# An explicit order of the attention words, a second order for the drain, and products of ones ahead of the experts

## The reference

```
x = x + layernorm(attention(layernorm(x)))
x = x + layernorm(ffn(layernorm(x)))
```

## Time and profile before

| | us |
|---|---|
| median of the runs shown | 1472.06 |
| the profiled execution | 1470.54 |
| its span, first to last instruction | 1468.8 |
| PE busy | 1219.1 (83%) |
| DVE busy | 954.1 (65%) |
| ACT busy | 721.2 (49%) |
| POOL busy | 836.0 (57%) |
| mean granted TensorE clock | 0.922 |
| chain that ended last | PE 56%, DVE 17%, POOL 8%, issue 8% |

### The profile page before, as it was taken

One profiled execution on the slowest core, in us unless ns is written; L12 is line 12 of the kernel. 1 busy time (PEld: TensorE's weight loads), 2 busy tenths in 40 slices (PEclk: granted clock), 3 DMA queues, 4 the chain that ended last, 5 costly groups with the idle time before them and its releaser, 6 DMA issues.

```text
span 1468.8 us, 27636 instructions
## 1 busy us (share of the span) xinstructions
PE 1219.1 (83%) x8581; PEld 700.7 (48%) x8581; DVE 954.1 (65%) x2397; ACT 721.2 (49%) x1521; POOL 836.0 (57%) x1047
## 2 busy tenths in 40 slices
PE   1479998989989898899988989988549999999920
PEld 0344554454554554545545455453325555555510
DVE  6388887778778677787777766752324444444467
ACT  0116665656556555565555564645214444444424
POOL 5425556657667476675756645545634555555557
PEclk9759999999999999999999998998668999999965
DMA  2431322321332213322132121431022334333256
GB/s 75 122 95 35 109 76 87 85 79 56 97 91 75 79 56 103 89 70 80 58 108 90 55 77 53 106 96 38 28 68 67 92 99 118 99 94 90 84 157 199
DMA packets 135287, 126.18 MB, mean 86 GB/s; under 512 B 17192, under 2 KB 126186, under 8 KB 130538
## 3 DMA queue, kind: packets, MB, share of 16 engines
q1 hardware_dynamic: 115360, 100.27, 23.9%
q0 software_dynamic: 8704, 18.11, 3.8%
q10 hardware_dynamic: 11082, 6.05, 1.6%
HBM read 78.12 MB, written 45.42 MB: 84 GB/s over the span
## 4 chain that ended last, share of the span: by engine, by line
PE 56%; DVE 17%; POOL 8%; issue 8%; ACT 3%; another core or an unknown queue 2%; DMA 1%; SPq 1%; POOLq 0%; DVEq 0%; ACTq 0%
PE wide L1556 6%; PE wide L1448 6%; DVE mx L1230 6%; PE score L1411 6%; PE heads_ps L1421 5%; PE wide L1538 4%; PE wide L1386 4%; PE score L1399 4%; PE score L1528 3%; POOL values L797 3%; PE wide L1557 2%; PE wide L1450 2%; DVE s_h L1171 2%; PE wide L1479 2%; ACT values L926 2%
## 5 line engine op out<-in xcount | busy, mean ns | idle before, releaser
L926 ACT ACTIVATE values<-score 128x512 f32<-128x512 f32 (+1 forms) x704 | 372.4, 558 | 250.6 <-PE score L1411 228.1
L1230 DVE TENSOR_REDUCE mx<-wide 128x2 f32<-128x1024 f32 (+3 forms) x384 | 390.1, 1038 | 127.7 <-PE wide L1450 113.1
L797 POOL TENSOR_SCALAR_AFFINE_SELECT values<-values 128x512 f32<-128x512 f32 x256 | 170.6, 670 | 321.7 <-ACT values L926 319.6
L1448 PE MATMUL wide<-qk 72*128 72x512 bf16 (+3 forms) x1024 | 248.1, 310 | 18.1 <-DVE mx L1230 15.9
L1411 PE MATMUL score<-qk 75*128 75x512 bf16 (+3 forms) x1024 | 241.1, 306 | 14.4 <-ACT values L926 10.7
L1421 PE MATMUL heads_ps<-values 128*32 128x512 f32 (+3 forms) x2048 | 194.1, 452 | 38.1 <-POOL values L797 37.1
L852 POOL DMA_INDIRECT token_scratch<-spread,e_id x144 | 140.9, 978 | 134.8 <-DVE spread L1275 81.8
L1450 PE MATMUL wide<-maskneg,identb 128*128 128x128 bf16 x1024 | 201.5, 225 | 0.0
L1411 PEld LDWEIGHTS score<-qk 75*128 75x128 bf16 x1024 | 82.5, 98 | 159.3 <-ACT values L926 73.9
L786 POOL DMA_INDIRECT sorted_scratch<-zr,places x128 | 131.7, 1029 | 27.3 <-issue 25.4
L1448 PEld LDWEIGHTS wide<-qk 72*128 72x128 bf16 x1024 | 103.1, 101 | 90.9 <-DVE mx L1230 37.1
(11 more groups left out here) (174 smaller groups left out, 1990.5 us busy)
## 6 DMA issues: line engine op xcount, KB each, us to landing
qk<-parts_scratch SPq DMA_DIRECT2D x192, 192.0 KB
parts_scratch<-spread SPq DMA_DIRECT2D x16, 768.0 KB, 8.4
qk<-sorted_scratch SPq DMA_DIRECT2D x144, 66.0 KB
front<-token_scratch SPq DMA_DIRECT2D x16, 512.0 KB, 4.1
xt<-attn_x SPq DMA_DIRECT2D x16, 256.0 KB, 8.7
xr<-attn_x SPq DMA_DIRECT2D x16, 256.0 KB, 8.9
x_scratch<-z SPq DMA_DIRECT2D x16, 256.0 KB, 4.6
shared_scratch<-s_out SPq DMA_DIRECT2D x16, 256.0 KB, 2.3
```

The costliest lines, as they stand in the source:

```text
L797: nc.gpsimd.affine_select(out=prob[n][:, :, 0:P], in_=prob[n][:, :, 0:P], compare_op=ALU.is_ge, fill=0.0, base=0, pattern=[[0, HG], [1, P] ...
L926: nc.scalar.activation(free_ap(prob[kb][:, hs_[0], :], [[1, N * len(hs_)]]), score[SCORE_RING.buffer(b, step)][:, 0:N * len(hs_)], ACT.Exp ...
L1230: nc.vector.tensor_reduce(mx[:, h0:h0 + len(hs_), j:j + 1], src, axis=AX.X, op=ALU.max).then_inc(p1_max, 1)
L1448: nc.tensor.matmul(o, q4[e][0:ROWS, h, j * P:(j + 1) * P], k4[e][0:ROWS, h, 0:L], start=True, stop=False)
```

## The change

The strings of `SLOTS` become one list, `ORDER`, with the group and number of each word spelled out and an offset of its own behind an @ where it differs. Iteration 16, which is now the last, follows a list of its own, `DRAIN`, in which the words of batches 14 and 15 stand in one sequence. The tables become words of that list (`counts`, `blocks`, `ends`, `rows`) and stand ahead of the last batch's shared expert; they use `heads_ps` and the score tiles and no longer the wide ones. SP stores the tails when the first of them is there and waits for the last ahead of the block loads.

The split of the maxima is done ahead of the transpose: DVE works on 128 x 32, PE brings the three bf16 parts across with three products with the identity, and ACT copies them to `mparts`. The bias of V is taken off V, multiplied with `Wp` and added to `bp` once at the start, so V's copy moves from DVE to ACT. `xnT` gets a third buffer. The fills of `k4` move from POOL to DVE, ahead of its wait for the weights, and the loads of expert weights from ACT's queue to SP's. The block tables and `e_xT` become views of `xnT`.

Ahead of the first expert block PE does 32 products of `onesb` with 512 columns, which nobody reads, and another 16 behind the wait for the first block's rows.

```diff
-SLOTS = [
-    "s0 last_v s1 X V last_heads s2 s3 late_p Q cos mask0 Y v0 s4 W s5 K s6 late_p sin0 s7 place sin1 late_p mask1 s8 "
-    "s9 U0 mask2 mask3 late_p G0 H0 v1 s10 zstats zrstd M1 v2",
-    "s0 s1 sin2 mask0 p s2 s3 p v3 d0 mask1 s4 s5 U1 sin3 p G1 s6 mask2 H1 v0 s7 mask3 Z p d1 s8 p s9 heads d2 stats s10 "
-    "v1 v2",
-    "s0 p p s1 U2 s2 p residual G2 s3 s4 p R mask0 H2 rstats s5 s6 v3 p p s7 s8 heads mask1 v0 s9 p p v1 rrstd s10 M0 "
-    "p mask2 rnormal T d3 mask3 v2",
-    "s0 s1 v3 p normal s2 s3 rX s4 p D rstd mask0 s5 p mask1 third0 s6 d4 third1 choose s7 v0 rL second p d5 mask2 s8 "
-    "heads mask3 p s9 d6 p chosen rexp s10 d7 v1 v2",
-]
-LATE = " ".join(SLOTS).split().count("late_p")
...
-FIRST, LAST = -4, 1
+ORDER = (
+    "sin0 s0.0 v3.2@-1 sin1 v3.3@-1 mask0.1 s0.1 X s0.2 chosen@-2 sin2 heads3@-1 p20@0 Q sin3 mask0.2 s0.3 s0.4 "
+    "p21@0 K s0.5 p22@0 d0 cos d1 s0.6 place s0.7 Y v0.0 s0.8 p23@0 s0.9 W mask0.3 s0.10 s1.0 U0 V v0.1 s1.1 M1@0 "
+    "zrstd zstats stats G0 s1.2 p0 v0.2 H0 s1.3 p1 mask1.0 residual v0.3 Z s1.4 U1 R s1.5 d2 p2 v1.0 G1 s1.6 p3 "
+    "s1.7 p4 s1.8 s1.9 p5 rstd s1.10 heads0 s2.0 p6 d3 s2.1 U2 rstats s2.2 G2 mask1.1 p7 s2.3 mask1.2 T v1.1 s2.4 "
+    "mask1.3 rrstd s2.5 second mask2.0 v1.2 p8 s2.6 p9 rnormal mask2.1 v1.3 s2.7 p10 mask2.2 s2.8 p11 v2.0 s2.9 "
+    "s2.10 third0 v2.1 s3.0 M0 normal H1 p12 p13 s3.1 v2.2 s3.2 mask2.3 rX mask3.0 heads1 s3.3 p14 s3.4 rL choose "
+    "v2.3 s3.5 s3.6 third1 H2 rexp mask3.1 p15 mask3.2 p16 mask3.3 v3.0 d4 s3.7 p17 s3.8 d5 heads2 s3.9 p18 s3.10 "
+    "p19 v3.1 d6 D d7 mask0.0@1 "
+)
+DRAIN = (
+    "v3.2@-1 v3.3@-1 chosen@-2 heads3@-1 K place Y d0 d1 W d2 d3 zstats U0 zrstd Z G0 U1 residual G1 rstats U2 "
+    "rrstd G2 rnormal rX rL choose rexp d4 d5 d6 d7 H0 H1 H2 D chosen K@-1 counts@-1 place@-1 blocks@-1 d0@-1 "
+    "d1@-1 d2@-1 d3@-1 d4@-1 d5@-1 d6@-1 d7@-1 U0@-1 ends@-1 U1@-1 rows@-1 U2@-1 G0@-1 G1@-1 G2@-1 H0@-1 H1@-1 "
+    "H2@-1 D@-1 "
+)
+OFFSET = dict(stats=4, rstd=4, normal=4, X=3, Q=3, cos=3, sin=3, R=3, T=3, second=3, third=3, V=1, p=1, M=1, s=0, v=0,
+              mask=0, heads=0, Y=-1, W=-1, zstats=-1, zrstd=-1, Z=-1, residual=-1, rstats=-1, rrstd=-1, rnormal=-1,
+              rX=-1, rL=-1, choose=-1, rexp=-1, chosen=-1, K=-2, place=-2, U=-2, G=-2, H=-2, D=-2, d=-2)
+FIRST, LAST = -4, 0
+GROUPED = ("s", "v", "mask", "heads")
...
+def schedule(text):
...
-        xnT = [sb(f"xnT{n}", [P, NT * P]) for n in range(2)]
+        xnT = [sb(f"xnT{n}", [P, NT * P]) for n in range(3)]
...
-        mrest = sb("mrest", [NH // 2 * NT, P])
+        mrest = sb("mrest", [P, NH // 2 * NT])
+        mpre = [sb(f"mpre{n}", [P, NPART, NH // 2 * NT], BF16) for n in range(2)]
+        bv_all = view(prob[3], F32, [P])
...
-            for n, v in enumerate((bq, bk, bv)):
+            for n, v in enumerate((bq, bk)):
+            sp.dma_start(bv_col[:], bv.rearrange("(h o) -> h o", o=1)).then_inc(weights_in, 16)
...
+                if i == B - 2:
+                    sp.wait_ge(qk_transposed, B)
+                    sp.dma_start(w2_sb[:, :, 0, :], w2[:, 0:HALF, :].rearrange("e h d -> h e d")).then_inc(w2_in, 16)
+                    sp.dma_start(w2_sb[:, :, 1, :], w2[:, HALF:, :].rearrange("e h d -> h e d")).then_inc(w2_in, 16)
+                if i == B - 1:
+                    sp.wait_ge(p2_scores, (B - 1) * P2_N * NG)
+                    sp.dma_start(w13_sb[:, :, 0:INTER], w1.rearrange("e d h -> d e h")).then_inc(w13_in, 16)
+                    sp.dma_start(w13_sb[:, :, INTER:], w3.rearrange("e d h -> d e h")).then_inc(w13_in, 16)
...
+            sp.wait_ge(p_done, 4)
...
-                if i == -3:
-
-                    pool.wait_ge(x_rstd, 1)
-                    for n in range(2):
-                        nc.gpsimd.memset(k4[n][64:96, :, :], 1.0).then_inc(rows_filled, 1)
-                        pool.wait_ge(rows_filled, n + 1)
-                for step in STEPS:
+                for step in (STEPS if i < B else REST):
...
+                    elif step.what == "M":
+                        act.wait_ge(max_transposed[n], b + 1)
+                        wait(act, m_in[n], 16 * NPART * b)
+                        nc.scalar.activation(mparts[n][:], misc[0:NH // 2 * NT, 0:NPART * P].rearrange("p (r c) -> p r c", r=NPART),
+                                             ACT.Copy).then_inc(m_ready[n], 1)
...
+                    elif step.what == "V":
+                        act.wait_ge(v_made, b + 1)
+                        if b == 0:
+                            act.wait_ge(filled, 4)
+                        wait(act, pv_done, (b - 1) * NG * NT)
+                        nc.scalar.activation(free_ap(vext[e][:, 0, 0, :], [[NH * 32, NT], [32, NH], [1, HS]]),
+                                             free_ap(unit[:, 0, :], [[P, NT], [HS, NH], [1, HS]]), ACT.Copy).then_inc(v_ready, 1)
-                        wait(act, v_made, b - 1)
-                        wait(act, qk_made, b)
-                        nc.scalar.activation(xnT[e][:], unit[:, 0, :], ACT.Copy).then_inc(xnT_ready, 1)
+                        wait(act, v_made, b - 2)
+                        wait(act, qk_made, b - 2)
+                        nc.scalar.activation(xnT[b % 3][:], unit[:, 0, :], ACT.Copy).then_inc(xnT_ready, 1)
...
+            for n in range(2):
+                nc.vector.memset(k4[n][64:96, :, :], 1.0).then_inc(rows_filled, 1)
+            nc.vector.tensor_copy(bv_all, free_ap(bv_col[:], [[0, P]])).then_inc(bv_spread, 1)
+            dve.wait_ge(bv_projected, 1)
+            nc.vector.tensor_tensor(bp_bc[:], bp_bc[:], misc[:, 0:P], ALU.add).then_inc(bp_folded, 1)
...
+            def tails_and_blocks():
+                nc.vector.tensor_tensor(tail_row[:], heads_ps[:, P:P + E], region[:], ALU.add).then_inc(p_done, 1)
...
+            def rows_and_experts():
...
-                    elif step.what == "V":
-                        dve.wait_ge(v_made, b + 1)
-                        wait(dve, pv_done, (b - 1) * NG * NT)
-                        nc.vector.tensor_tensor(
-                            free_ap(vext[e][:, 0, 0, :], [[NH * 32, NT], [32, NH], [1, HS]]),
-                            free_ap(unit[:, 0, :], [[P, NT], [HS, NH], [1, HS]]),
-                            free_ap(bqkv_bc[:], [[0, NT], [HS, NH], [1, HS]], 2 * P), ALU.add).then_inc(v_ready, 1)
...
-                        dve.wait_ge(max_transposed[n], b + 1)
-                        wait(dve, m_in[n], 16 * NPART * b)
-                        mt, mp = misc[0:NH // 2 * NT, 0:P], mparts[n]
-                        ms[n].did(nc.vector.tensor_scalar(mp[:, 0, :], mt, -1.0, None, ALU.mult))
+                        dve.wait_ge(p1_max, b * P1_N + (n + 1) * P1_N // 2)
+                        wait(dve, max_transposed[n], b)
+                        m, mp = mx[:, n * NH // 2:(n + 1) * NH // 2, :].rearrange("p h t -> p (h t)"), mpre[n]
+                        ms[n].did(nc.vector.tensor_scalar(mp[:, 0, :], m, -1.0, None, ALU.mult))
...
-                        nc.vector.tensor_tensor(mp[:, 2, :], mrest[:], mp[:, 1, :], ALU.subtract).then_inc(m_ready[n], 1)
+                        nc.vector.tensor_tensor(mp[:, 2, :], mrest[:], mp[:, 1, :], ALU.subtract).then_inc(m_split[n], 1)
...
+                    elif step.what == "counts":
+                        pe.wait_ge(heads_copied, B * NG)
+                        counts = chosen[B % 2][:, NK, :]
+                        nc.tensor.matmul(heads_ps[0:E, 0:1], counts, onesb[:, 0:1], start=True, stop=True)
+                        nc.tensor.matmul(heads_ps[:, P:P + E], onesb[:], counts, start=True, stop=True).then_inc(p_total, 1)
+                    elif step.what == "ends":
+                        pe.wait_ge(p_blocks, 1)
+                        pe.wait_ge(p_done, 1)
+                        nc.tensor.matmul(heads_ps[0:E, 2 * P:2 * P + 1], upto[:], nblk_b[:], start=True, stop=True).then_inc(p_ends, 1)
+                    elif step.what == "rows":
+                        pe.wait_ge(p_past, 1)
+                        pe.wait_ge(exp_done, B * NG * P2_N)
+                        pe.wait_ge(s_out_ready, B - 1)
+                        for o, w in ((score[0], onesb[0:E, :]), (score[1], spare_b[:])):
+                            last = nc.tensor.matmul(o[:, 0:NBLK], w, past[:], start=True, stop=True)
+                        last.then_inc(p_experts, 1)
...
-                        pe.wait_ge(p1_max, b * P1_N + (n + 1) * P1_N // 2)
-                        apart(pe)
-                        nc.tensor.transpose(misc[0:NH // 2 * NT, 0:P],
-                                            mx[:, n * NH // 2:(n + 1) * NH // 2, :].rearrange("p h t -> p (h t)"),
-                                            ident[:]).then_inc(max_transposed[n], 1)
+                        if b == 0 and n == 0:
+                            pe.wait_ge(bp_folded, 1)
+                        pe.wait_ge(m_split[n], b + 1)
+                        for r in range(NPART):
```

(25 more changed lines are left out.)

105 lines of the change are left out of this document (37 added, 68 removed).

## The result

| | before | after |
|---|---|---|
| median, us (7 runs each) | 1467.08 | 1452.04 |
| profiled execution | 1470.54 | 1447.03 |
| its span | 1468.8 | 1445.3 |
| PE / DVE / ACT / POOL busy in it | 83 / 65 / 49 / 57% | 84 / 67 / 51 / 57% |

The ratio is 0.9906 (95% interval 0.9883 to 0.9928): the gain is clear of the noise, but under the 2% from which two kernels are called different, so the verdict is "same". Some executions of either kernel fall in a slower state (1689 and 1695 us of the seven before); they stay in the medians and out of the ratios. Forecast was 1434; the time lies in the range, the gain is under half of the forecast one. The profiled execution of after is the fastest of its seven, so its span is 23.5 shorter where the medians differ by 15.

The account below looks back on a forecast made before the run. PE bounds the loop only in part: 5.3 us of a batch idle, mostly behind POOL's masks and DVE's maxima. 1470.5 - 32 (loop) - 2.5 (start) - 3.3 (entry) = 1432.7; the median lies 1.5 higher: 1434, range 1390 to 1473.

Parts of the forecast that it names:

- The loop, -2.3 a full batch: Attention loop: -1.2 from DVE, -1.6 from POOL, +0.5 for D make -2.3 us a full batch, -32 in all.
- A batch that still takes 60: Sign in the loop that the forecast is wrong; copies out of the shared experts were to come every 58.4 us.
- D at the end, 0.5 given back: Shared experts' down product, last in the order, keeps PE busy 3 us with one exp queued on ACT: +0.5 a batch.
- rival (D): Slower: in the loop D holds PE, the next score waits for its copy; 3 a batch, 1507 us, chance 0.10.
- POOL, -1.6: Loop: of 2.6 us a batch that PE idles behind POOL's masks, 1.6 goes as masks stand ahead of scatters.
- DVE, -1.2 of 1.9: Loop: smaller splits and V's bias take 1.9 us a batch off DVE; 1.2 of PE's idle comes back.
- PE's work stays: Loop: PE does the same words; three bf16 products replace each f32 transpose of the maxima, +0.1 a batch, within rounding.
- The last batches, -8.0: Batch 12's first exp to the last value product's end: 2.8 full batches and one lighter, -8.0 us in all.
- The start, -2.5: Start: k4 fills on DVE, two taking 14.1 us by elements; first normalisation ends at 25.0 against 27.5, -2.5.
- Drain and entry, -3.3: Last value product to first expert blocks: blocks in 7.2 us earlier, first transpose -1.4, faster first blocks -1.9.
- The products of ones: Ahead of the first expert block: 32 cost 6.9 us and 16 cost 3.5 at full clock, and buy 1.9.
- (C): Rival for the loop: waits only move and the lighter DVE alone counts; 1457 us, up to 1472, chance 0.30.

Follow-up runs that it names:

- a1: The changed kernel itself, unchanged, on another chip, with no signal late: 1390.3 us, 0.960 of the kernel before.
- e1: The changed kernel with D (shared experts' down product and its copy) two scores earlier in the repeated order: 1408.9 us, 0.975 of the kernel before.
- e5: The changed kernel with the old order written out as the list, on the chip where the kernel before takes 1470: 1590.2 us, 1.085 of it.
- e2: The changed kernel with scatters d4 to d7 spread over GpSimd's idle stretches, D left last: 1413.5 us, 0.979 of the kernel before.
- e3: The changed kernel with U1 moved ahead of the residual and normal behind rX: 1372.5 us, 0.951 of the kernel before.
- e4b: e4 run once more, on the chip of a1: 1382.3 us, 0.955 of the kernel before.
- e4: The changed kernel with the two k4 fills on VectorE as 4096 4-byte words each instead of 8192 2-byte ones: 1381.1 us, 0.955 of the kernel before.
- c2: c1 with another drain list (H0 to H2 earlier among the scatters, K of the last batch ahead of D): 1359.1 us, 0.941 of the kernel before.
- c1: The changed kernel with the edits of e3 and e4 together, run twice: 1362.7 and 1363.1 us, 0.942 and 0.946 of the kernel before.
- a0: The changed kernel itself once more, on the chip where the kernel before takes 1470: 1455.3 us, 0.992 of the kernel before.
- b0: The kernel before, unchanged, once more, on the same chip as a0: 1469.7 us.
- b1: The kernel before, unchanged, on a chip without late signals: 1441.7 us, one execution.

## Why the forecast was off

**The loop, -2.3 a full batch, came out at +0.1 in the result (60.7 to 60.8).** This is the step that failed, by two of its terms: D, given 0.5, and the gain of a lighter DVE, given 1.2. Without late signals 2.3 came (58.6 to 56.3), but that the number fits is luck, for the terms came out otherwise than written: 2.6 instead of 1.6 from POOL, 0.6 from a wait for exps that the sum didn't have, nothing for D, and 0.9 lost behind the maxima where 1.2 was to be won. A batch that still takes 60 is what the forecast named as its own sign of being wrong.

*D at the end, 0.5 given back.* This term failed by its size. PE idled 2.6 to 2.8 behind D in seven of the nine full batches from 252 to 799, and the clock fell behind it. The forecast had this in rival (D), with its place and its price of 3 a batch, but weighed it at 0.10; the copy alone takes 0.6. What made it 2.8 is PE's late signals. They are in the trace of before too, where ACT's copy `oT` waited for a value product long ended:

```profile
434.07 0.43 PE L1421 MATMUL heads_ps<-values 128*32 128x128 f32 x8
...
437.03 0.60 ACT L932 ACTIVATE oT<-heads_ps 128x512 f32<-128x512 f32 x1 [2.26 <-remote]
```

There only `heads` stood behind it. "Remote" on an idle of 2 us whose producer ended before was the thing to ask about. Moving D there put the copy, a score tile and the next score behind the same late signals. Without late signals the place costs nothing: a1 has no idle behind D, and e1 is slower than a1. Whether an earlier D is the better one on the slower chip was not run. What holds the signals is not settled. In both kernels, and in e5, it comes where scatters stand on POOL and SP issues its large transfers; but a1 has the same scatters and transfers and nothing late, so they are not enough by themselves. e2 was to part these and never met the chip.

*POOL, -1.6.* Right, and more: the waits of value products for masks, 23.2 us from 252 to 798 before (2.6 a batch), are 0 after.

*DVE, -1.2 of 1.9.* This term failed by its sign, with late signals and without: PE's waits for the maxima went from 1.8 to 2.7 a batch. The sizes were right: the split's instructions take 0.17 to 0.19 each. But others grew. DVE, then POOL beside it, at two places of the batch:

```profile
475.13 3.28 DVE L1071 TENSOR_SCALAR xn<-xt,mv,rstd 128x128 f32<-128x128 f32 x4
478.32 2.34 DVE L1245 TENSOR_REDUCE mx<-wide 128x2 f32<-128x1024 f32 x2
...
475.93 1.15 POOL L835 TENSOR_TENSOR spread<-spread 128x512 bf16<-128x512 f32 x1
477.04 1.27 POOL L788 TENSOR_TENSOR s_aT<-s_h,s_g 128x512 f32<-128x512 f32 x1
```
```profile
456.72 2.66 DVE L1193 SCALAR_TENSOR_TENSOR s_h<-s_th,s_h 128x512 f32<-128x512 f32 x1
...
456.45 2.38 POOL L826 TENSOR_TENSOR front<-front 128x1024 f32<-128x1024 f32 x1
```

The four instructions of `normal` take 1.1 together where POOL is idle. That of `U1` takes 2.66 instead of 0.68 beside POOL's part of `R`. The row maxima take 1.22 and 0.95 in both lists, whatever POOL does. The Trainium skill (SBUF — State Buffer, Who interferes with whom) says that VectorE and GpSimd share a pair of ports, which an instruction holds to its end: `tensor_scalar` from and to SBUF can need it, and so can one with two SBUF inputs, a `tensor_reduce` never. The trace agrees: `normal` is of the first kind and `U1` of the second, and the maxima are reductions, though they read PSUM and so don't test the rule in SBUF. I should have laid POOL's words of the new list beside DVE's with that rule. e3 took `normal` out of the collision: its `xn` fell from 0.88 to 0.34 an instruction, DVE's batch from 47.9 to 44.9, PE's wait ahead of rX went, and a batch takes 54.1 instead of 56.3 at a clock of 1.00. The other half of e3 missed: U1 still met R, at 2.52, so I put the gain down to `normal`; the two weren't run apart. One full batch of e3:

```profile
413.10:467.20 54.10, 52.53 (x445) 30.90 (x441) 44.91 (x107) 35.63 (x69) 38.27 (x45) 1.00 0.31 90
```

*PE's work stays.* Right in microseconds, wrong in what it leaves out: `M` on PE now waits for the split. e5 shows the price that the new list hides: 5.4 of idle in a batch of 68.3. Neither the order nor the move off DVE can be priced alone.

**The last batches, -8.0, came out at -24.7.** The forecast took them for full batches, the last one for a full one with fewer words. In truth it is another problem: with few maxima left PE reaches the value products sooner, and in the old list POOL is later still. Nothing in the forecast foresaw the 16.7 us beyond its 8.0; without them the two medians would hardly differ. That there is a gain at all in the result is luck. The waits of PE from 798.5 in before, from 799 in after:

```profile
PE heads_ps L1421 <- POOL values L797: 11.3, 11, 3.0
PE score L1411 <- ACT values L926: 3.7, 7, 1.1
PE misc L1429 <- ACT oT L932: 2.3, 2, 1.6
```
```profile
PE score L1429 <- ACT s_out L967: 5.2, 2, 2.7
PE score L1429 <- ACT values L929: 1.9, 5, 0.6
PE wide L1468 <- DVE mx L1245: 1.5, 1, 1.5
```

By the windows above PE idles 11.8 instead of 24.0, and its same work takes 196.8 instead of 209.3, at a clock of 0.96 for 0.93. So 12.2 of the 24.7 are idle and 12.5 shorter busy time. By the two clocks about half of the 12.5 is the clock's (my estimate, 209.3 x 0.03 / 0.96 = 6.5); the rest isn't explained.

**The start, -2.5, came out at +0.8.**

```profile
5.35 0.22 DVE L1036 MEMSET values<- 128x64 f32 x2
7.33 6.88 DVE L1039 MEMSET qk<- 32x8192 bf16 x1 [1.76 <-issue]
15.87 6.88 DVE L1039 MEMSET qk<- 32x8192 bf16 x1 [1.66 <-issue]
22.79 0.23 DVE L1041 COPY values<-bv_col 128x128 f32<-128x128 f32 x1
```
```profile
6.47 3.47 DVE L1040 MEMSET qk<- 32x4096 f32 x1 [0.91 <-DVE values L1037]
10.75 3.47 DVE L1040 MEMSET qk<- 32x4096 f32 x1 [0.80 <-issue]
```

The first fence is the changed kernel, the second e4b. A fill ends 8.54 after the one before it (from 14.21 to 22.75), not 6.88: the 1.66 of "issue" in front belongs to it. That is 1.04 ns an element, and 4.27 for 4096 in e4b is the same; the fill of 2048 in the earlier trace rows starts 2.14 before its like, 1.04 again. I took the duration where the distance of two in a row was to be read. The Trainium skill (VectorE: DVE Perf Modes, Zero memsets can be issued as uint32) had it right at one cycle per element. What the forecast worked out from it, 17 us the pair and no gain at the start, came true (17.08 by the distance of the ends); I set it aside on the strength of the row's duration. Its advice to fill by 4 bytes speaks of zeros; e4 does the same with a pair of bf16 ones as one f32, and the first normalisation ends at 19.8 instead of 28.4.

**Drain and entry, -3.3, came out at +0.7.** The blocks were to be in 7.2 sooner; the last copy of D ended 63.4 after T0 where 58.2 was reckoned, and the 5.2 stay in all that follows. The chain by its rows:

```profile
1031.33 1.09 PE L1475 MATMUL wide<-ident,zr 128*128 128x128 f32 x4 [9.03 <-POOL zr L758]
1040.09 1.86 PE L1482 MATMUL wide<-gw_sb,hT 128*128 128x16 f32 x8 [7.67 <-ACT hT L949]
1042.41 5.49 PE L1417 MATMUL score<-sw_sb,s_aT 128*128 128x128 f32 x24
...
1037.63 0.68 ACT L957 ACTIVATE s_h<-wide,sb_half 96x512 f32<-96x512 f32 x1 [16.03 <-POOL s_aT L788]
...
1039.35 0.59 ACT L949 ACTIVATE hT<-wide 128x512 f32<-128x512 f32 x1
```

rX stood 23.7 after T0, not 20: the signal of the last value product was late by 2, and POOL's residual took 2.24 beside DVE instead of 1.27. Then `hT` waited 7 us on ACT behind U2 of batch 14, U2 for H0, and H0 for four scatters on POOL. The forecast followed POOL and PE and did not walk ACT's queue for `hT`. c2 takes that chain out: 6.7 sooner for `hT` than in c1, 3.8 for the last copy of D.

The products of ones: they ran at the full clock (10.5 for 48, as assumed; 12.16 in a1) and the first blocks too. Their return is 3.4 to 3.5 in two pairs of traces, where I had 1.9. They still cost 4.5 to 7.6.

**Of the rivals**, (C), the waits only move, at 1457 and a chance of 0.30, comes nearest. It is right on the full batches of the result, where new waits filled the place of the old. It had nothing of the last ones, and on the other chips the loop did get shorter.

## What to carry to other kernels

An idle labelled "remote", on an engine whose producer ended long before, can be a late signal: find out what stands behind it before a tile's release is moved there, and if a gain hangs on it, measure on more than one chip. When an order is rewritten, lay the words of VectorE that go from SBUF to SBUF against the wide words of GpSimd at the same place, and walk every queue of the drain, ScalarE's too. A batch of the loop's end is not a full batch with fewer words; what its engines wait for is read in its own window.

## What the runs showed of the hardware that I had not expected

The same program, with the same instructions at the same distances, has PE's signals late once a batch on one chip, mostly by 2.2 to 3.1 us, and on time on four others. Meanwhile DVE's semaphores went up on time: in a0 that of its last reduction (L1122), which ends 0.83 after D, follows by 0.01 wherever it is recorded. The 59.2 us between the spans of a0 (1450.3) and a1 (1391.1) lie in the loop, where the late signals are. By the medians the difference between the chips is 62 us of 1452 for the changed kernel and 18 to 25 of 1467 for the one before, and the ratio of the two moved from 0.960 to 0.991. That all of it comes from the late signals is argued, not shown.

One rival is not ruled out. The traces of the slower chip lack a good part of the engines' semaphore records: 744 of 7805 in a0, 692 of 7802 in b0, and likewise 746 and 698 in the two traces of the result; a1 lacks 9 and b1 26. Every time on record has a recorded span beside it. So it may be the recording that holds PE's signals on that chip, and no run shows what the kernels take there without it.
